# Two edge stages of a graph network: keys and values of a tile four chunks sooner, the second layer's closing steps of a tile in fewer steps

## The chip, the cores and the metric

The kernel runs on one core of a Trainium2 chip. The metric is the device time of one execution in microseconds. Before the change three runs took 2850.37, 2851.22 and 2853.70 us; the median is 2851.22.

A core has engines with a queue of instructions each, which run in order and meet through semaphores: PE (TensorE, matmuls and turns of 128x128 blocks), DVE (VectorE), ACT (ScalarE), POOL (GpSimd) and SP (SyncE). In this kernel POOL issues gathers of table rows, SP issues most other loads, and ACT the stores of the edge stages.

## The reference, cut to what matters

6250 nodes with 256 features, 100000 edges sorted by target and one loop per node. `x` is normalised to `xn`; two graph attention layers with 4 heads follow, and beside them one linear attention without softmax, whose keys and values are normalised per head:

```python
def gat_conv(x, src, dst, W, a_src, a_dst, b):
    h = (x @ W).reshape(-1, H, C)
    e = leaky_relu(alpha_s[src] + alpha_d[dst], 0.2)
    ex = exp(e - segment_max(e, dst)[dst])
    alpha = ex / segment_sum(ex, dst)[dst]
    return segment_sum(h[src] * alpha[:, :, None], dst).reshape(-1, H * C) + b
x0 = relu(gat_conv(xn, src, dst, W1, ...))
x2 = gat_conv(x0, src, dst, W2, ...)

k, v = _inst_norm_lastdim(k), _inst_norm_lastdim(v)      # 8 heads of 64
dots = einsum('bhnd,bhne->bhde', k, v)
out = einsum('bhnd,bhde->bhne', q, dots) / n             # then Wout, + bout

x = x + x2 + out
x = x + _L0_ffn_ref(_layernorm(x))                       # 16 experts, best 2, gate logits x @ gate_w
```

## The kernel before, in words

The program is a row of stages with a barrier of all engines behind each. Two of them, one per layer, are built by `gat_edges` (L771) and are the stages that the change touches. In between stands a short stage that bounds the logits; after the second layer come the ordering of tokens by expert, the experts and the last norm.

An edge stage walks 98 chunks of 1024 edges; two chunks go with one tile of 128 nodes, so there are 49 tiles. For a chunk SP loads its source numbers (`load`, L902) and the targets' codes (`load_codes`, L908), POOL gathers 8 x 128 table rows into one of three slots (L950), PE fetches the targets' terms (`targets`), DVE forms the logits (`edge_logits`, L1009), ACT their exponentials (`exps`, L1143), DVE scales the gathered rows (`edge_scale`, L1028), PE adds them up by target (`add`, L1266), and DVE puts the sums into the accumulator (`gain`, L1036). POOL's gather of a chunk waits until the scaling of the chunk three before it is done. A few matmuls without use (L1250, L1258) fill pauses of PE.

For each tile further steps follow. In both layers DVE takes the reciprocal of the denominators (`denominators`, L1045) and ACT divides (`divide`, L1156). Then, in the first layer, PE turns the result (`fin_turn`, L1296), ACT applies relu (L1176), PE projects it for the second layer (`project`, L1302), ACT copies it out (`copies`, L1184) and stores it. Beside that runs a second row of steps which depends on the node's own features alone: load of the transposed rows (`load_x`, L920), values and keys on PE (L1274, L1280), squares on ACT (L1164), sums on DVE (L1061), square roots on ACT (L1170), scaled keys on DVE (L1070) and their products with the values, summed over all tiles on PE (`dots`, L1288). When all tiles are through, DVE and PE make the mixing matrix from the products (L1080 to L1085, L1313, L1318). In the second layer PE mixes (`mix`, L1326 to L1329: features, mixing matrix, bias and the divided sums in one bank), DVE takes the statistics (`stats`, L1091) and keeps a copy (`with_beta`, L1098), ACT takes the root (L1203), DVE makes the factors (`scales`, L1102), ACT normalises (`normalise`, L1209) and stores, PE turns the tile (`fin_turn`, L1335), ACT copies it (`xf_turned`, L1214), PE computes the gate logits (`gates`, L1342), and ACT copies these out (L1218). When the last are there, DVE adds the gate's bias (L1113) and picks the experts.

The order on each engine is written by `chunks` (L858) with `skewed` (L90). Each engine has a list of pairs of an offset and a step. At time t of its own program it runs, in the list's order, each step for chunk t - offset; a step marked `True` belongs to tiles and runs only where t - offset is even. Head and tail are written out, six chunks in the middle make the body of a loop. So an offset sets beside which chunk's steps a step stands, and the list sets the order inside a chunk; semaphores do the rest.

Of the kernel before, what the change touches and what calls it, by code (L numbers as in the profile page):

```python
# [56 lines left out]
def hold(eng, sem, value, tick):  # L57

    eng.wait_ge(sem, value)
    eng.sem_inc(tick, 1)  # L60
# [24 lines left out]
def rows_of(i):  # L85

    return LAST if isinstance(i, int) and i == NT - 1 else P


def skewed(eng, n, period, head, tail, stages):  # L90

    most, least = max(o for o, _ in stages), min(o for o, _ in stages)
    start = head + most
    turns = max(0, n - tail + least - start) // period

    def whole(t):  # L100
        for o, step in stages:
            if 0 <= t - o < n:
                step(t - o, (t - o) % period, (t - o) // period)
    for t in range(min(least, 0), start):
        whole(t)
    if turns:
        with eng.Fori(0, turns) as m:  # L107
            for r in range(period):
                for o, step in stages:
                    k = start + r - o  # L110
                    step(m * period + k, k % period, m + k // period)
    for t in range(start + turns * period, n + most):
        whole(t)
# [657 lines left out]
def gat_edges(nc, layer, srcp, table, idx, G, ahead, codes_d, partition, iota, acc, own, peak, parts, windows, attention, last, sem):  # L771
# [6 lines left out]
    with ExitStack() as ctx:  # L778
# [79 lines left out]
        def chunks(eng, begin, end, *stages):  # L858


            rounds = eng.value_load(passes[0:1, 0:1], min_val=1, max_val=NT + 1)
            with eng.Fori(0, rounds) as r:
                def told(step):
                    return lambda c, k, u: step(r * NC + c, c, k % SLOTS, k % 2, r * len(range(k % SLOTS, NC, SLOTS)) + u * 2 + k // SLOTS)

                def tile_of(step):

                    def even(c, k, u):
                        if k % 2 == 0:
                            b = k // 2  # L870
                            step(r * NT + (u * SLOTS + b), u * SLOTS + b, b, r * len(range(b, NT, SLOTS)) + u)
                    return even
                begin(r)
                skewed(eng, NC, 2 * SLOTS, 2, 2, [(o, tile_of(step) if by_tile else told(step)) for o, step, *by_tile in stages])
                end(r)
            return rounds
# [4 lines left out]
        def new_pass(eng):  # L881
            return lambda r: hold(eng, s["pass"], r * 3 + 3, s["tick"])

        def new_dest(eng):
            return lambda r: hold(eng, s["dests"], r + 1, s["tick"])

        def both_new(eng):
            def begin(r):
                new_pass(eng)(r)
                new_dest(eng)(r)  # L890
            return begin
# [4 lines left out]
        @block.sync  # L896
        def _(sp):
            def next_load(r):
                hold(sp, s["logits"], r * NC + NC + SLOTS, s["tick"])
                sp.dma_start(idx[:, 0, :], srcp[0:CE].rearrange("(p t) -> p t", t=KT)).then_inc(s["idx_in0"], 16)  # L900

            def load(g, c, q, par, use):  # L902
                if isinstance(c, int) and c == 0:
                    return
                hold(sp, s["logits"], g + 1, s["tick"])
                sp.dma_start(idx[:, q, :], srcp[ds(c * CE, CE)].rearrange("(p t) -> p t", t=KT)).then_inc(s[f"idx_in{q}"], 16)

            def load_codes(g, c, q, par, use):  # L908
                hold(sp, s["hotT"], g + 1, s["tick"])
                sp.dma_start(codes[:, par, :], codes_d[ds(c * CE, CE)].rearrange("(o e) -> o e", o=1).to_broadcast([P, CE])).then_inc(s[f"codes_in{par}"], 16)  # L910

            sp.sem_inc(s["stored"], PER_STORE)
            if attention:
                for kc in range(2):
                    sp.dma_start(bias[:, kc:kc + 1], a["L0_gnn_b1"][kc * P:(kc + 1) * P].rearrange("(p o) -> p o", o=1)).then_inc(s["constants"], 16)

                def load_x(t, i, b, use):
                    sp.wait_ge(s["values_ps"], t + 1)
                    sp.wait_ge(s["keys_ps"], t + 1)
                    sp.dma_start(xnT[b], xnT_d[ds(i, 1), :, :].rearrange("o p f -> (o p) f")).then_inc(s[f"xn_in{b}"], 16)  # L920

                rounds = chunks(sp, new_pass(sp), next_load, (0, load), (-1, load_codes), (1, load_x, True))
            else:
                sp.dma_start(bias[0:1, 0:C], a["L0_gnn_b2"].rearrange("(o c) -> o c", o=1)).then_inc(s["constants"], 16)
                sp.dma_start(bias[0:1, C:2 * C], a["L0_mix_bout"].rearrange("(o c) -> o c", o=1)).then_inc(s["constants"], 16)
                sp.dma_start(beta, a["L0_ffn_beta"].rearrange("(o c) -> o c", o=1).to_broadcast([P, C])).then_inc(s["constants"], 16)
                sp.dma_start(gate, a["L0_ffn_gate_w"].rearrange("(k p) e -> p k e", p=P)).then_inc(s["constants"], 16)
                for rows in (xf_d, moe_d):
                    sp.dma_start(rows[NT * P:(NT + 1) * P, 0:C], mixM[:, 0, :]).then_inc(s["constants"], 16)
                sp.dma_start(gbias, a["L0_ffn_gate_b"].rearrange("(o e) -> o e", o=1).to_broadcast([P, NX])).then_inc(s["constants"], 16)  # L930

                def load_x(t, i, b, use):
                    n = rows_of(i)
                    sp.wait_ge(s["mixed"], t + 1)
                    sp.dma_start(x[b][0:n, :], a["x"][ds(i * P, n), :]).then_inc(s[f"x_in{b}"], 16)
                    sp.dma_start(xnT[b], xnT_d[ds(i, 1), :, :].rearrange("o p f -> (o p) f")).then_inc(s[f"x_in{b}"], 16)

                rounds = chunks(sp, new_pass(sp), next_load, (0, load), (-1, load_codes), (6, load_x, True))
            hold(sp, s["stored"], rounds * (PER_STORE * NT) + PER_STORE, s["tick"])

        @block.gpsimd
# [34 lines left out]
        def _(dve):  # L976
# [81 lines left out]
            if attention:  # L1058
# [13 lines left out]
                key = Chain(dve, s["key"])  # L1072
                dve.sem_inc(s["kvsum"], 1)
                dve.sem_inc(s["ks"], 1)
                rounds = chunks(dve, both_new(dve), next_pass, (1, edge_logits), (1, placed), (1, edge_scale), (6, keys, True), (-1, one_hot), (3, gain), (5, denominators, True), (5, sums, True))

                hold(dve, s["dots"], rounds * NT + SLOTS, s["tick"])
                for hp in range(4):
# [7 lines left out]
            else:  # L1086
# [20 lines left out]
                dve.wait_ge(s["constants"], 112)  # L1107
                dve.tensor_tensor(bias[0:1, 0:C], bias[0:1, 0:C], bias[0:1, C:2 * C], ALU.add).then_inc(s["bias"], 1)
                dve.memset(acc[:, NT + 2, :], 4.0).then_inc(s["yb"], 1)
                rounds = chunks(dve, both_new(dve), next_pass, (1, edge_logits), (1, placed), (8, scales, True), (1, edge_scale), (-1, one_hot), (3, gain), (5, denominators, True), (7, stats, True), (7, with_beta, True))  # L1110

                hold(dve, s["gate_logits"], rounds * NT + 1, s["tick"])
                steps.link(dve.tensor_tensor(logits, logits, gbias.rearrange("p (t e) -> p t e", t=1).to_broadcast([P, NT, NX]), ALU.add))  # L1113
# [24 lines left out]
        def _(act):  # L1138
# [20 lines left out]
            if attention:  # L1159
# [31 lines left out]
                act.sem_inc(s["vs"], 1)  # L1191
                act.sem_inc(s["out"], 4)
                act.wait_ge(s["constants"], 32)
                chunks(act, new_dest(act), nothing, (9, store, True), (6, roots, True), (1, exps), (6, divide, True), (5, squares, True), (7, relu, True), (8, copies, True))
            else:
                act.wait_ge(s["codes_in1"], 16)
                act.wait_ge(s["idx_in2"], 16)
# [26 lines left out]
                act.sem_inc(s["xf"], 1)  # L1224
                act.sem_inc(s["xfT"], 1)
                act.sem_inc(s["gate_logits"], 1)
                chunks(act, new_dest(act), nothing, (9, store, True), (8, root, True), (1, exps), (13, gates, True), (11, xf_turned, True), (6, divide, True), (8, normalise, True))
                act.wait_ge(s["gap"], 1)
                act.activation(gap[:], gap[:], ACT.Exp).then_inc(s["exp"], 1)

# [1 line left out]
        def _(pe):  # L1232
# [19 lines left out]
            def after_placed(n):  # L1252

                def step(g, c, q, par, use):
                    pe.wait_ge(s["acc"], g * 2 + 2)
                    pe.wait_ge(s["hotf"], g + 1)
                    for _ in range(n):
                        pe.matmul(psA[:, q, 0:C], ident[:], wext[:, 0, 0:C] if attention else mixM[:, 0, :], start=True, stop=True)  # L1258
                return step
# [9 lines left out]
            if attention:  # L1269
# [29 lines left out]
                def project(t, i, b, use):  # L1299
                    pe.wait_ge(s["relu"], t + 1)  # L1300
                    for kc in range(2):
# [3 lines left out]
                pe.sem_inc(s["values_ps"], SLOTS)  # L1305
                pe.sem_inc(s["keys_ps"], SLOTS)
                pe.sem_inc(s["projected"], 1)
                chunks(pe, nothing, nothing, (1, targets), (2, add), (7, fin_turn, True), (7, dots, True), (8, project, True),
                       (1, after_logits), (5, keys, True), (4, values, True), (1, after_placed(2)))

                pe.wait_ge(s["end"], 8)
                for hp in range(4):
# [7 lines left out]
            else:  # L1320
# [17 lines left out]
                def gates(t, i, b, use):  # L1338
                    pe.wait_ge(s["xfT"], t + 2)
                    pe.wait_ge(s["gate_logits"], t + 1)  # L1340
                    for kc in range(2):
# [3 lines left out]
                pe.sem_inc(s["gated"], 1)  # L1345
                pe.wait_ge(s["constants"], 112)
                pe.wait_ge(s["bias"], 1)
                chunks(pe, nothing, nothing, (1, targets), (2, add), (12, gates, True), (10, fin_turn, True), (7, mix, True),
                       (1, after_logits), (1, after_placed(3)))


# [464 lines left out]
```

## Time and profile before

| | us |
|---|---|
| median of 3 runs | 2851.22 |
| profiled execution | 2856.6 |
| its span | 2855.0 |
| first edge stage, first gather to mixing matrix | 189.91 to 1211.14 |
| second edge stage, first gather to last gate logits | 1238.42 to 2257.66 |
| POOL busy | 1867.3 (65%) |
| PE busy | 2212.2 (77%) |
| DVE busy | 1832.7 (64%) |
| ACT busy | 924.3 (32%) |

The span is the time from the first to the last instruction of the profiled execution. A share is a mean over all stages, which are bound by different engines; the two edge stages make up over 2000 of the 2855 us.

### The profile page before, as it was taken

The page shows a single profiled execution, that of the slowest core. Times are in us where ns is not written, and L with a number is a line of the kernel's source. Part 1 is how long each engine was busy: PE and PEld are TensorE (multiplying, and loading weights), DVE is VectorE, ACT ScalarE, POOL GpSimd, SP SyncE. Part 2 cuts the span into 40 slices and gives each one's busy share as a digit, 9 for nine tenths or more (in the row PEclk, how much of TensorE's full clock was granted, in tenths as well). Part 3 has the DMA queues.
Part 4 walks back from the last instruction along what each step waited for, and adds up shares of the span by engine and source line. Part 5 has one row for each costly group of instructions (what it writes and reads, how often), then busy time and mean ns, then how long its engine had stood idle before and what let it go on. Part 6 is the DMA issues. An engine that isn't in the chain of part 4 may idle for free. (4 is left out here: it accounts for less than half of the span.)

```text
span 2855.0 us, 54407 instructions
## 1 busy us (share of the span) xinstructions
PE 2212.2 (77%) x11635; PEld 1734.9 (61%) x11636; DVE 1832.7 (64%) x4388; ACT 924.3 (32%) x2254; POOL 1867.3 (65%) x1934
## 2 busy tenths in 40 slices
PE   1727787777777787737888888888888569999986
PEld 0525555555555555536666666666666359999985
DVE  5656767777777777566666666666666475555546
ACT  0512333333333333301222222222222244444436
POOL 0247777777777777467777777777777116666654
PEclk9969999999999999969999999999999679999998
DMA  3735555555555555255555565555565255555545
GB/s 70 221 107 141 147 147 147 147 145 145 145 145 146 145 149 142 74 193 157 158 161 161 156 161 154 162 154 162 157 163 158 70 150 103 103 104 104 101 86 187
DMA packets 274988, 401.57 MB, mean 141 GB/s; under 512 B 91136, under 2 KB 187799, under 8 KB 274905
## 3 DMA queue, kind: packets, MB, share of 16 engines
q0 software_dynamic: 102496, 253.89, 36.1%
q1 hardware_dynamic: 128745, 101.18, 13.4%
q10 hardware_dynamic: 43680, 45.76, 4.9%
q8 instruction: 24, 0.39, 0.1%
q14 instruction: 43, 0.35, 0.0%
HBM read 346.42 MB, written 54.62 MB: 140 GB/s over the span
## 5 line engine op out<-in xcount | busy, mean ns | idle before, releaser
L950 POOL DMA_INDIRECT gathered<-table,idx x1568 | 1501.5, 958 | 508.0 <-issue 451.5
L1266 PE MATMUL psA_e<-scaled,hotf 128*128 128x260 f32 x3136 | 745.8, 391 | 43.5 <-issue 38.9
L1266 PEld LDWEIGHTS psA_e<-scaled,hotf 128*128 128x128 f32 x3136 | 587.6, 192 | 132.7 <-issue 47.9
L1146 ACT ACTIVATE scaled<-t_e 128x32 f32<-128x32 f32 x196 | 45.0, 230 | 735.6 <-DVE t_e L1017 734.6
L1679 POOL DMA_INDIRECT moe_d<-xscaled,xtarget x113 | 179.3, 1587 | 125.8 <-DVE xtarget L1623 53.7
L1028 DVE TENSOR_TENSOR scaled<-gathered,psDW_e 128x2048 f32<-128x2048 f32 x98 | 223.5, 2281 | 25.7 <-ACT psDW_e L1147 25.7
L1021 DVE TENSOR_TENSOR hotf<-psA_e,code_r 128x1024 f32<-128x1024 f32 x196 | 239.6, 1222 | 0.0
L1028 DVE TENSOR_TENSOR scaled<-gathered,psW_e 128x2048 f32<-128x2048 f32 x98 | 223.5, 2280 | 22.8 <-ACT psW_e L1147 22.8
L1651 PEld LDWEIGHTS xpsH<-xxT,w1e 128*128 128x128 f32 x1808 | 221.1, 193 | 6.2 <-ACT xxT L1580 0.4
L1660 PE MATMUL xpsO<-w,hidT 128*128 x904 | 217.5, 384 | 9.2 <-DVE hidT L1612 9.0
L1651 PE MATMUL xpsH<-xxT,w1e 128*128 128x128 f32 x1808 | 221.8, 276 | 0.0
L1250 PE MATMUL psD_e<-mixM,ident 128*128 128x256 f32 x392 | 121.3, 437 | 117.2 <-DVE t_e L1017 117.0
L1036 DVE SCALAR_TENSOR_TENSOR acc<-psA_e,lower,acc 128x260 f32 x196 | 95.7, 488 | 151.6 <-issue 151.3
L1612 DVE TENSOR_SCALAR hidT<-xpsH,b1T 128x128 f32<-128x128 f32 x452 | 127.3, 344 | 93.6 <-issue 43.3
L1660 PEld LDWEIGHTS xpsO<-w,hidT 128*128 128x128 f32 x904 | 163.3, 191 | 31.8 <-issue 13.4
L1258 PE MATMUL psA_e<-mixM,ident 128*128 128x256 f32 x588 | 177.4, 446 | 5.0
L1015 DVE TENSOR_TENSOR z_e<-both_e,gathered 128x32 f32<-128x32 f32 x196 | 37.8, 193 | 218.4 <-DMA gathered<-table,idx 209.6
L1146 ACT ACT_TABLE_LOAD x95 | 121.9, 1283 | 171.8 <-DVE t_e L1017 142.7
L1250 PEld LDWEIGHTS psD_e<-mixM,ident 128*128 128x128 f32 x392 | 75.9, 207 | 143.0 <-DVE t_e L1017 134.3
L1258 PEld LDWEIGHTS psA_e<-mixM,ident 128*128 128x128 f32 x588 | 127.2, 225 | 47.2 <-issue 26.9
L1280 PE MATMUL psKV<-w 128*128 128x512 f32 x196 | 102.0, 645 | 65.2 <-DVE t_e L1017 65.1
L1274 PE MATMUL psKV<-w 128*128 128x512 f32 x196 | 99.2, 629 | 66.6 <-DVE t_e L1017 66.6
(322 smaller groups left out, 3372.1 us busy)
## 6 DMA issues: line engine op xcount, KB each, us to landing
w<-codes_d SPq DMA_DIRECT2D x196, 256.0 KB
gathered<-table,idx POOLq DMA_INDIRECT x1584
w<-in_L_ffn_w ACTq DMA_DIRECT2D x8, 2048.0 KB, 19.8
xb<-in_L_ffn_b SPq DMA_DIRECT2D x113, 128.0 KB
table<-acc POOLq DMA_DIRECT2D x49, 130.0 KB
table<-acc ACTq DMA_DIRECT2D x49, 130.0 KB
xnT_d<-xnT ACTq DMA_DIRECT2D x49, 128.0 KB, 1.8
w<-xnT_d SPq DMA_DIRECT2D x49, 128.0 KB
```

Of the source, the lines that this page charges most:

```text
L950: pool.indirect_dma_start(out=G[:, q, k, :], out_offset=None, in_=table, in_offset=bass.IndirectOffsetOnAxis(ap=idx[:, q, k:k + 1], axis=0 ...
L1021: dve.tensor_tensor(hotf[:, q, :, :], psA[:, q, 512 - P:512].rearrange("p (k f) -> p k f", k=1).to_broadcast([P, KT, P]), code_r[:, ds(c * ...
L1028: dve.tensor_tensor(scaled[:, par, :, 0:C].rearrange("p k (h c) -> p k h c", h=H), f, w, ALU.mult).then_inc(s["scaled"], 1)
L1146: act.activation(scaled[:, par, :, C:GW], t[:], ACT.Exp).then_inc(s["weights"], 1)
L1250: pe.matmul(psD_bank[:, 256:256 + C], ident[:], mixM[:, 0, :], start=True, stop=True)
L1258: pe.matmul(psA[:, q, 0:C], ident[:], wext[:, 0, 0:C] if attention else mixM[:, 0, :], start=True, stop=True)
L1266: ins = pe.matmul(psA[:, q, 0:GW], hotf[:, q, k, :], scaled[:, par, k, :], start=(k == 0), stop=(k == KT - 1))
L1280: ins = pe.matmul(psKV[:, 0, :], xnT[b][:, kc * P:(kc + 1) * P], wkvT[:, kc, 0, :], start=(kc == 0), stop=(kc == 1))
L1612: dve.tensor_scalar(hidT[:, q % 2, k * P:(k + 1) * P], psH[:, q % 2, k * P:(k + 1) * P], b1T[:, ds(e, 1), k:k + 1].rearrange("p o k -> p ( ...
L1651: ins = pe.matmul(psH[:, q % 2, k * P:(k + 1) * P], w1e[:, q % 2, kc, k * P:(k + 1) * P], xT[:, q % 2, kc, :], start=(kc == 0), stop=(kc = ...
L1660: ins = pe.matmul(psO[:, q % 2, 0:C], hidT[:, q % 2, k * P:(k + 1) * P], w2[:, ds(e, 1), k, :].rearrange("p o f -> p (o f)"), start=(k == ...
L1679: pool.indirect_dma_start(out=moe_d, out_offset=bass.IndirectOffsetOnAxis(ap=target[:, q % 2:q % 2 + 1], axis=0), in_=scaled[:, q % 2, :], ...
```

## The change

It alters only offsets and, in one list, the order; no operation is added, dropped or resized.

First layer: the offset of each of the eight steps of keys and values falls by four chunks: loading 1 to -3, values 4 to 0, keys, squares and sums 5 to 1, roots and scaled keys 6 to 2, products 7 to 3. Dividing, turning, relu, projecting, copying and storing stay.

Second layer: loading 6 to 4, mixing 7 to 6, statistics and copy 7 to 6, roots, scales and normalising 8 to 7, store 9 to 8, turn 10 to 9, copy of the turned tile 11 to 9, gates on PE 12 to 10, gates on ACT 13 to 11. The division keeps 6. On ACT, division and copy of the turned tile now stand ahead of the exponentials of the same time, where they stood behind.

```diff
 # SP, first and second layer
-(0, load), (-1, load_codes), (1, load_x, True)
+(0, load), (-1, load_codes), (-3, load_x, True)
-(0, load), (-1, load_codes), (6, load_x, True)
+(0, load), (-1, load_codes), (4, load_x, True)
 # DVE, first and second layer
-(1, edge_logits), (1, placed), (1, edge_scale), (6, keys, True), (-1, one_hot), (3, gain), (5, denominators, True), (5, sums, True)
+(1, edge_logits), (1, placed), (1, edge_scale), (2, keys, True), (-1, one_hot), (3, gain), (5, denominators, True), (1, sums, True)
-(1, edge_logits), (1, placed), (8, scales, True), (1, edge_scale), (-1, one_hot), (3, gain), (5, denominators, True), (7, stats, True), (7, with_beta, True)
+(1, edge_logits), (1, placed), (7, scales, True), (1, edge_scale), (-1, one_hot), (3, gain), (5, denominators, True), (6, stats, True), (6, with_beta, True)
 # ACT, first and second layer
-(9, store, True), (6, roots, True), (1, exps), (6, divide, True), (5, squares, True), (7, relu, True), (8, copies, True)
+(9, store, True), (2, roots, True), (1, exps), (6, divide, True), (1, squares, True), (7, relu, True), (8, copies, True)
-(9, store, True), (8, root, True), (1, exps), (13, gates, True), (11, xf_turned, True), (6, divide, True), (8, normalise, True)
+(8, store, True), (7, root, True), (6, divide, True), (9, xf_turned, True), (1, exps), (11, gates, True), (7, normalise, True)
 # PE, first and second layer
-(1, targets), (2, add), (7, fin_turn, True), (7, dots, True), (8, project, True), (1, after_logits), (5, keys, True), (4, values, True), (1, after_placed(2))
+(1, targets), (2, add), (7, fin_turn, True), (3, dots, True), (8, project, True), (1, after_logits), (1, keys, True), (0, values, True), (1, after_placed(2))
-(1, targets), (2, add), (12, gates, True), (10, fin_turn, True), (7, mix, True), (1, after_logits), (1, after_placed(3))
+(1, targets), (2, add), (10, gates, True), (9, fin_turn, True), (6, mix, True), (1, after_logits), (1, after_placed(3))
```

How the instructions stand, at three places. On SP at the start of the first layer's edge stage, before (L910 loads codes, L906 source numbers, L920 transposed rows):

```order
L59 ISA
L910 DMA w<-codes_d 128x1024
L59 REGISTER_ALU
L910 DMA w<-codes_d 128x1024
L906 DMA idx<-srcp 128x8
```

and now:

```order
L918 ISA
L920 DMA w<-xnT_d 128x256
L59 ISA
L910 DMA w<-codes_d 128x1024
L918 REGISTER_ALU
L920 DMA w<-xnT_d 128x256
L59 REGISTER_ALU
L910 DMA w<-codes_d 128x1024
L906 DMA idx<-srcp 128x8
```

Two loads of transposed rows stand ahead of the first load of source numbers; the one that stood behind it is now for a later tile.

On PE at the end of the same stage, after the last chunk's rows were added up, before (psKV are keys and values, psF turned and projected tiles, psM the products):

```order
L1294 ISA
L1296 MATMUL psF<-ident,w 128x128 x2
L1288 MATMUL psM<-w 128x128 x4
L1280 MATMUL psKV<-w 128x512 x2
L1302 MATMUL psF<-wext,w 128x264 x2
L1271 ISA
L1272 REGISTER_ALU
L1274 MATMUL psKV<-w 128x512 x2
```

and now, from the same turn to the barrier:

```order
L1294 ISA
L1296 MATMUL psF<-ident,w 128x128 x2
L1284 REGISTER_ALU
L1288 MATMUL psM<-w 128x128 x4
L1302 MATMUL psF<-wext,w 128x264 x2
L1294 ISA
L1296 MATMUL psF<-ident,w 128x128 x2
L1302 MATMUL psF<-wext,w 128x264 x2
```

Keys and values of the last tiles no longer stand between the turns and the projections; one set of products is left there, and it is the last tile's.

On ACT in the second layer's loop, before (L1203 roots, L1146 and L1147 exponentials, L1156 division, L1214 copy of the turned tile, L1218 gate logits):

```order
L1218 ISA
L1218 ACTIVATE w<-psG 128x16
L1213 REGISTER_ALU
L1214 ACTIVATE w<-psX_1 128x256
L1203 ACT_TABLE_LOAD
L1203 ACTIVATE w<-w,eps 128x1
L1144 ISA
L1145 REGISTER_ALU
L1146 ACT_TABLE_LOAD
L1146 ACTIVATE scaled<-t_e 128x8x4
L1147 ACTIVATE psW_e<-t_e 128x32
```

and now:

```order
L1203 ACT_TABLE_LOAD
L1203 ACTIVATE w<-w,eps 128x1
L1214 ACTIVATE w<-psX_1 128x256
L1144 ISA
L1145 REGISTER_ALU
L1146 ACT_TABLE_LOAD
L1146 ACTIVATE scaled<-t_e 128x8x4
L1147 ACTIVATE psW_e<-t_e 128x32
L1218 ISA
L1218 ACTIVATE w<-psG 128x16
```

The copy of the turned tile stands between the root and the table load of the next exponentials; the gate logits stand behind these.

## Rows read from the trace of the kernel before

**Rows 1.** Groups by line, first edge stage, 240:1160 us: busy, mean | idle.

```profile
L950 POOL DMA_INDIRECT gathered<-table,idx x733 | 696.9, 951 | 223.4 <-issue 210.0 <-DVE scaled L1028 12.2 <-DMA idx<-srcp 1.2
```

**Rows 2.** The same view, second edge stage, 1300 to 2190 us.

```profile
L950 POOL DMA_INDIRECT gathered<-table,idx x709 | 674.3, 951 | 216.1 <-issue 205.1 <-DVE scaled L1028 8.2 <-DMA idx<-srcp 2.7
```

**Rows 3.** Waits of DVE, 1300 to 2190 us: total, times, longest.

```profile
DVE z_e L1015 <- DMA gathered<-table,idx: 99.8, 41, 4.0
```

**Rows 4.** Timeline, one tile of the second layer: start, length, engine, line [idle before].

```profile
1741.91 1.28 ACT L1146 ACT_TABLE_LOAD   x1 [1.72 <-DVE t_e L1017]
...
1743.20 0.23 ACT L1146 ACTIVATE scaled<-t_e 128x32 f32<-128x32 f32 x1
...
1743.56 2.29 DVE L1028 TENSOR_TENSOR scaled<-gathered,psW_e 128x2048 f32<-128x2048 f32 x1 [0.32 <-ACT psW_e L1147]
...
1750.04 1.03 PE L1326 MATMUL psY<-mixM,w1e 128*128 128x256 f32 x4
...
1752.29 0.38 ACT L1214 ACTIVATE w<-psX 128x256 f32<-128x256 f32 x1
...
1752.59 1.03 PE L1250 MATMUL psD_e<-mixM,ident 128*128 128x256 f32 x4
...
1752.73 2.27 DVE L1028 TENSOR_TENSOR scaled<-gathered,psW_e 128x2048 f32<-128x2048 f32 x1
...
1755.11 3.75 PE L1266 MATMUL psA_e<-scaled,hotf 128*128 128x260 f32 x16
...
1758.63 0.18 DVE L1045 RECIPROCAL rden<-acc 128x4 f32 x1 [0.99 <-DVE acc L1036]
...
1758.69 0.52 PE L1342 MATMUL psG<-w 128*128 128x16 f32 x4
...
1759.05 0.42 PE L1335 MATMUL psX<-ident,w 128*128 128x128 f32 x2
```

**Rows 5.** Timeline, end of the first layer's edge stage.

```profile
1180.65 0.38 PE L1296 MATMUL psF<-ident,w 128*128 128x128 f32 x2
...
1183.68 1.02 ACT L1164 ACTIVATE w<-psKV 128x1024 f32<-128x1024 f32 x1 [8.60 <-PE psKV L1280]
...
1189.24 0.49 DVE L1036 SCALAR_TENSOR_TENSOR acc<-psA_e,lower,acc 128x260 f32 x1 [0.61 <-issue]
...
1197.95 0.69 PE L1296 MATMUL psF<-ident,w 128*128 128x128 f32 x2 [1.53 <-ACT dtab L1185]
...
1198.71 0.62 ACT L1176 ACTIVATE w<-psF,w 128x128 f32<-128x128 f32 x2 [0.81 <-PE psF L1296]
...
1200.14 1.97 PE L1302 MATMUL psF<-wext,w 128*128 128x264 f32 x4
...
1202.37 0.39 ACT L1184 ACTIVATE acc<-psF 128x260 f32 x1 [3.04 <-PE psF L1302]
...
1210.45 0.69 DVE L1085 COPY mixM<-psM 128x512 f32<-128x512 f32 x1 [3.81 <-PE psM L1318]
```

**Rows 6.** Timeline, end of the second layer's edge stage.

```profile
2235.87 2.05 PE L1326 MATMUL psY<-mixM,w1e 128*128 128x256 f32 x4 [3.21 <-ACT w L1209]
...
2243.24 1.06 ACT L1156 ACTIVATE w<-acc,rden 128x64 f32 x4 [0.94 <-DVE acc L1098]
...
2244.90 2.05 PE L1326 MATMUL psY<-mixM,w1e 128*128 128x256 f32 x4 [2.66 <-ACT w L1209]
...
2252.41 0.56 ACT L1209 ACTIVATE w<-psY,w 128x256 f32<-128x256 f32 x1 [1.07 <-DVE w L1104]
...
2256.41 1.03 PE L1342 MATMUL psG<-w 128*128 128x16 f32 x4 [0.47 <-ACT w L1214]
...
2257.81 0.97 DVE L1113 TENSOR_TENSOR w<-w 128x784 f32<-128x784 f32 x1 [4.36 <-ACT w L1218]
```

**Rows 7.** Timeline, start of the first layer's edge stage.

```profile
184.90 13.43 DVE L992 TENSOR_TENSOR acc<-acc 128x3136 f32<-128x3136 f32 x4 [0.43 <-ACT acc L1141]
...
189.91 2.65 POOL L950 DMA_INDIRECT gathered<-table,idx  x1 [6.70 <-DMA idx<-srcp]
```

More of the change, by code:

```diff
@@ L920, in load_x @@
                     sp.dma_start(xnT[b], xnT_d[ds(i, 1), :, :].rearrange("o p f -> (o p) f")).then_inc(s[f"xn_in{b}"], 16)
-                rounds = chunks(sp, new_pass(sp), next_load, (0, load), (-1, load_codes), (1, load_x, True))
+                rounds = chunks(sp, new_pass(sp), next_load, (0, load), (-1, load_codes), (-3, load_x, True))
             else:
@@ L936, in load_x @@
                     sp.dma_start(xnT[b], xnT_d[ds(i, 1), :, :].rearrange("o p f -> (o p) f")).then_inc(s[f"x_in{b}"], 16)
-                rounds = chunks(sp, new_pass(sp), next_load, (0, load), (-1, load_codes), (6, load_x, True))
+                rounds = chunks(sp, new_pass(sp), next_load, (0, load), (-1, load_codes), (4, load_x, True))
             hold(sp, s["stored"], rounds * (PER_STORE * NT) + PER_STORE, s["tick"])
@@ L1074, in _ @@
                 dve.sem_inc(s["ks"], 1)
-                rounds = chunks(dve, both_new(dve), next_pass, (1, edge_logits), (1, placed), (1, edge_scale), (6, keys, True), (-1, one_hot), (3, gain), (5, denominators, True), (5, sums, True))
+                rounds = chunks(dve, both_new(dve), next_pass, (1, edge_logits), (1, placed), (1, edge_scale), (2, keys, True), (-1, one_hot), (3, gain), (5, denominators, True), (1, sums, True))
                 hold(dve, s["dots"], rounds * NT + SLOTS, s["tick"])
@@ L1109, in _ @@
                 dve.memset(acc[:, NT + 2, :], 4.0).then_inc(s["yb"], 1)
-                rounds = chunks(dve, both_new(dve), next_pass, (1, edge_logits), (1, placed), (8, scales, True), (1, edge_scale), (-1, one_hot), (3, gain), (5, denominators, True), (7, stats, True), (7, with_beta, True))
+                rounds = chunks(dve, both_new(dve), next_pass, (1, edge_logits), (1, placed), (7, scales, True), (1, edge_scale), (-1, one_hot), (3, gain), (5, denominators, True), (6, stats, True), (6, with_beta, True))
                 hold(dve, s["gate_logits"], rounds * NT + 1, s["tick"])
@@ L1193, in _ @@
                 act.wait_ge(s["constants"], 32)
-                chunks(act, new_dest(act), nothing, (9, store, True), (6, roots, True), (1, exps), (6, divide, True), (5, squares, True), (7, relu, True), (8, copies, True))
+                chunks(act, new_dest(act), nothing, (9, store, True), (2, roots, True), (1, exps), (6, divide, True), (1, squares, True), (7, relu, True), (8, copies, True))
             else:
@@ L1226, in _ @@
                 act.sem_inc(s["gate_logits"], 1)
-                chunks(act, new_dest(act), nothing, (9, store, True), (8, root, True), (1, exps), (13, gates, True), (11, xf_turned, True), (6, divide, True), (8, normalise, True))
+                chunks(act, new_dest(act), nothing, (8, store, True), (7, root, True), (6, divide, True), (9, xf_turned, True), (1, exps), (11, gates, True), (7, normalise, True))
                 act.wait_ge(s["gap"], 1)
@@ L1307, in _ @@
                 pe.sem_inc(s["projected"], 1)
-                chunks(pe, nothing, nothing, (1, targets), (2, add), (7, fin_turn, True), (7, dots, True), (8, project, True),
-                       (1, after_logits), (5, keys, True), (4, values, True), (1, after_placed(2)))
+                chunks(pe, nothing, nothing, (1, targets), (2, add), (7, fin_turn, True), (3, dots, True), (8, project, True),
+                       (1, after_logits), (1, keys, True), (0, values, True), (1, after_placed(2)))
                 pe.wait_ge(s["end"], 8)
@@ L1347, in _ @@
                 pe.wait_ge(s["bias"], 1)
-                chunks(pe, nothing, nothing, (1, targets), (2, add), (12, gates, True), (10, fin_turn, True), (7, mix, True),
+                chunks(pe, nothing, nothing, (1, targets), (2, add), (10, gates, True), (9, fin_turn, True), (6, mix, True),
                        (1, after_logits), (1, after_placed(3)))
```

## Prediction

> **What bounds the kernel now.** I read the busy shares at the head of the profile first: POOL is busy 65%, PE 77%, DVE 64%, and none of them is full over the span. So I asked stage by stage, with the groups by line. Both edge stages belong to POOL. In 920 us of the first, 733 indirect gathers took 696.9 us, and POOL's idle time of 223.4 us is almost all "issue", about 0.3 us between one gather and the next [rows 1]; 696.9 + 223.4 = 920.3, which is the whole window. In 890 us of the second it is 674.3 + 216.1 = 890.4 [rows 2]. One gather costs 890.4 / 709 = 1.256 us, so a chunk (8 gathers) 10.05 us and a tile (two chunks) 20.1 us. POOL waited for DVE for 8.2 us in all there. DVE, on the other side, waited 99.8 us for gathered rows [rows 3]: about 2.2 us for each of some 44 tiles. So DVE, ACT and PE follow, and a step moved among them costs nothing as long as their own circle closes within 20.1 us per tile and a chunk is freed before POOL comes back to its slot three chunks later.
>
> What POOL doesn't cover are the two ends, after the last gather, where the steps of the last tiles run one after another, and the first microseconds of a stage. There the change can give or take.
>
> **The change, part by part.** *First layer, inside the stage.* Load, values, keys, squares, sums, roots, key scaling and products of a tile all move by the same four chunks, an even number, so each keeps its neighbours in a chunk's list on every engine. Each chunk still holds the same instructions, for a tile two further on. No DMA is added; only the tile that it loads differs. Cost 0, hidden under POOL [rows 1].
>
> *First layer, end.* Before, keys and values of the last two tiles are computed after the last gather, between the output steps of tiles 46 to 48. ACT stood 8.60 us until the key matmul of tile 47 let it square [rows 5]; the turned hidden state of tile 46 was ready soon after 1180.65 and waited behind that. The sums for tile 47 also held DVE in its queue, so the last chunk's accumulation came at 1189.24. The turn of tile 48 starts at 1197.95, the end of the stage is the mixing matrix at 1210.45 + 0.69 = 1211.14. Afterwards none of that stands there, and one tile's round remains: turn 0.69, relu 0.62, projection 1.97, copies (0.39 and a small one, about 0.46 together), with some 0.45 of hand-overs, 4.2 us with PE at the lower of its two clock levels, as in these rows, and about 3.1 us at the upper, at which the turn took 0.38 [rows 5]. Two rounds from 1180.65 to 1181.8 (up to 1.1 later if the last accumulation on PE runs at the lower clock, since the value matmul before it goes) put the turn of tile 48 at 1187 to 1190, middle 1188.7: 9.2 us sooner. Behind it, the products (L1288) of tile 48 go from between relu, which ended at 1199.33, and projection at 1200.14: 0.8 us. The final products and copies after that stay. Sum 10 us; bounds 7 and 12.
>
> *First layer, start.* SP now issues two loads of transposed rows (128 KB each) ahead of the first index load, on which POOL's first gather waited until 189.91 [rows 7]. With 256 KB more in front of it, beside two code lists of 256 KB each that stand there already, I estimate that list 1 to 2 us later. That gather, 2.65 us long, stood under four DVE multiplies of 13.43 / 4 = 3.36 us each that began at 184.90: it ended at 192.56, 0.94 (a usual gather's length, 951 ns in [rows 1]) after the boundary between the second and third at 191.62, as if it had only run in the gap. If it still starts before 191.62, nothing is lost, otherwise one gather, 1.25 us; both ends are kept and I take 0.6.
>
> *Second layer, inside the stage.* Here steps change parity, and a new circle forms: the division (ACT) feeds the mixing of the same chunk (PE), which stands before that chunk's filler matmuls and so before the next accumulation; behind that comes the turn, and the copy of the turned tile now stands on ACT ahead of the next exponentials, for which DVE's scaling waits. From the reciprocal's end R [rows 4, 6]: hand-over 0.2, division 1.06, hand-over 0.1; mixing to filler 1752.59 - 1750.04 = 2.55; filler to accumulation 1755.11 - 1752.59 = 2.52; accumulation to the next step 1758.69 - 1755.11 = 3.58; turn 0.42 and hand-over 0.05; copy 0.38; from the exponential's table load to the scaling 1743.56 - 1741.91 = 1.65; from the scaling to the end of the next reciprocal 1758.81 - 1752.73 = 6.08. Sum 18.6 us against 20.1. It closes with 1.5 to spare, so POOL keeps the pace and I cost it at 0. Before, the circle left about 2.2 [rows 3]. Behind the waiting copy stand the exponentials, a gate copy and the normalising; behind the waiting mixing the fillers and the next targets. Without POOL's cover each us over 20.1 costs 1 us in each of some 45 tiles. Below zero there is nothing either: POOL isn't sped up.
>
> On the table load the Trainium skill, ScalarE: Activation LUTs, section What ACT_TABLE_LOAD costs, speaks against the change: 1283 ns and a drain of about 1380 ns for every switch. The trace shows the 1.28, and the exponential at 1743.20, 0.01 behind its end [rows 4]; no drain is seen. With the drain the circle would be an estimated 20.0, and nothing left.
>
> *Second layer, end.* Mixing of tile 47 started at 2235.87, of tile 48 at 2244.90, its normalised rows were ready at 2252.41 + 0.56 = 2252.97, and the logits were complete at 2257.81 [rows 6]: 4.84 us in which PE did the gate of tile 47, the turn of 48 and the gate of 48, with an ACT copy before each gate. Afterwards the copy and gate of 47 come before the normalising, and behind it remain one turn (0.7, as in [rows 5]), one copy (0.38), one gate (1.03) and hand-overs: 2.6. That is 2.2 less. Mixing of tile 47 starts up to 2 us sooner, for its division no longer waits for the tile before to be scaled, but then scales, reciprocal, normalising and store lie between it and the next division, so I keep only 0.5 of it. Sum 2.7; bounds 1 and 4. In these rows PE is at the lower level, 1.2 GHz: L1326 takes 2.05 for 1.03 in [rows 4]. I leave it so.
>
> **Sum.** -10 + 0.6 - 2.7 = -12.1 us. The profiled execution took 2856.6 (span 2855.0), so 2844.5 on its own scale. It lies 5.4 over the median of the runs, 2851.2; the same difference taken from the median gives 2839.1.
>
> **Rivals.** *A: the circle of the second layer becomes the bound (slower).* Place: ACT's exponentials behind the turned copy, DVE's scaling behind these. It decides from 20.1 us per tile, that is 1.5 over my sum. For it: mixing at the lower clock takes twice 2.55, which alone makes it 21.2, and PE now has a pause before each mixing, from the gate's end to the division's, about 1 us. Against: that pause is shorter than the 3.21 us before the slow L1326 [rows 6]. Price: 1.1 x 45 = 50 us, 2889; with half of the tiles at the lower clock the mean is 19.9 and nothing is lost. By the Trainium skill's drain (same section of ScalarE: Activation LUTs) the half-slow case would be an estimated 21.3 and 2893; with no drain in the rows it has 0.02 of A's chance.
>
> *B: keys and values didn't matter at the first end.* The output steps of the last tiles could be as long without them, since projection, copies and turn form a chain of their own; then only the second end counts: 2851.2 + 0.6 - 2.7 = 2849. For it: the last three rounds are serial anyway. Against: the 8.60 us.
>
> *C: half of it comes back.* PE, less busy, runs all of the first end at the lower clock, the index load costs a whole gather, and the second end gives 1: -7 + 1.3 - 1 = -6.7, 2844.5.
>
> **How the numbers follow.** What a measurement here can tell from no change is about 0.2%, 5.7 us. My forecast has 0.60 and C 0.14, both faster; B has 0.12 and is no change, A 0.14 and is slower. Faster 0.74, same 0.12, slower 0.14. The likeliest case is 2839, with its own range 2836 to 2845. To 2852 it takes in B; only A, and ends that are better than both bounds, lie outside.
>
> **What would show it.** Gathers in the middle of both stages at 1.256 us each as before, and DVE still waiting for gathered rows in the second layer, though less than 2.2 us per tile. No squares on ACT behind the first layer's last scaling, and the mixing matrix about 10 us closer to it. At the second end one gate behind the last normalising. POOL waiting for DVE's scaling in the middle of the second layer, or the time from last gather to mixing matrix unchanged, would prove me wrong.

## The result, and the profile of the changed kernel

The changed kernel takes 2870.48 us (median of 4 runs, 2865.11 to 2871.92), the kernel before 2851.06 (4 runs). The ratio is 1.006, with a 95% interval of 1.0048 to 1.0073: slower, where 2839 was predicted. The profiled execution took 2865.11 us (span 2863.5).

The first layer did what was forecast. Groups by line, 240 to 1160 us, as in [rows 1]:

```profile
L950 POOL DMA_INDIRECT gathered<-table,idx x735 | 697.0, 948 | 223.9 <-issue 211.1 <-DVE scaled L1028 11.3 <-DMA idx<-srcp 1.5
```

Timeline of its start and end (start, length, engine, line, what is done, idle time before), as in [rows 5, 7]:

```profile
191.22 1.32 POOL L950 DMA_INDIRECT gathered<-table,idx  x1 [8.02 <-DMA idx<-srcp]
192.85 2.98 POOL L950 DMA_INDIRECT gathered<-table,idx  x1 [0.31 <-issue]
...
1187.16 0.69 PE L1296 MATMUL psF<-ident,w 128*128 128x128 f32 x2 [0.77 <-ACT dtab L1185]
...
1199.04 0.69 DVE L1085 COPY mixM<-psM 128x512 f32<-128x512 f32 x1 [3.81 <-PE psM L1318]
```

Before, the second gather stood at the same place:

```profile
192.86 2.98 POOL L950 DMA_INDIRECT gathered<-table,idx  x1 [0.31 <-issue]
```

The gathers keep their pace, and nothing is lost at the start. The turn of the last tile is at 1187.16 where it was at 1197.95, and the mixing matrix at 1199.04 where it was at 1210.45: 11.4 us sooner. So the 19 us that were lost lie behind it, and 11 more that were given away there.

Groups by line, 1300 to 2190 us, as in [rows 2]:

```profile
L950 POOL DMA_INDIRECT gathered<-table,idx x697 | 660.3, 947 | 230.6 <-issue 206.2 <-DVE scaled L1028 21.0 <-DMA idx<-srcp 3.4
```

Twelve gathers fewer in the same 890 us, and longer waits for VectorE, 21.0 us for 8.2. The waits of DVE there (total, times, longest), as in [rows 3]:

```profile
DVE both_e L1012 <- issue: 88.5, 15, 7.5
...
DVE scaled L1028 <- ACT psW_e L1147: 36.0, 41, 1.5
...
DVE z_e L1015 <- DMA gathered<-table,idx: 10.7, 7, 2.3
```

DVE waited 99.8 us for gathered rows before and 10.7 now. In their place stand 88.5 us, in 15 times, for nothing that the profile shows ("issue"); before, that row held 2.7. Thirteen of the fifteen are long, 6.3 to 7.5 us with a mean of 6.8. One of them, in the timeline of DVE:

```profile
1623.52 0.42 DVE L1098 TENSOR_TENSOR acc<-psY,w 128x256 f32 x1 [0.60 <-issue]
1630.27 0.36 DVE L1012 TENSOR_REDUCE both_e<-psD_e 128x64 f32<-128x192 f32 x1 [6.33 <-issue]
1630.87 0.19 DVE L1015 TENSOR_TENSOR z_e<-both_e,gathered 128x32 f32<-128x32 f32 x1 [0.24 <-DVE both_e L1012]
```

The next one ends at 1692.23, the fifth of such a row (from 1506.13) at 1754.57, so one comes every 62.1 us: once in 6 chunks, which is one pass through the loop that `skewed` builds on DVE (called a turn of the loop from here on; it has nothing to do with the turn of a tile). Each stands at that loop's back branch: ahead of it ran the last step of the loop's body (L1098), behind it the first (L1012). The DMA queues from 1300 to 2190 us (queue: packets, MB, share) say what goes on then; q14 is the queue that loads instructions:

```profile
q14 instruction: 70, 0.57, 0.2%
```

The kernel before moved 7 such packets in the same 890 us. From one stall to the next there are five, and three of the five fall into the stall itself (1624 to 1630.3 us in the one shown). So instructions of the loop are fetched anew in each turn.

The second end, as in [rows 6]:

```profile
2241.79 1.07 ACT L1156 ACTIVATE w<-acc,rden 128x64 f32 x4 [1.84 <-issue]
...
2252.76 1.06 ACT L1156 ACTIVATE w<-acc,rden 128x64 f32 x4 [1.76 <-issue]
...
2261.41 0.56 ACT L1209 ACTIVATE w<-psY,w 128x256 f32<-128x256 f32 x1 [0.73 <-DVE w L1104]
...
2264.91 0.97 DVE L1113 TENSOR_TENSOR w<-w 128x784 f32<-128x784 f32 x1 [2.46 <-ACT w L1218]
```

From the last normalising's end to the logits it is 2.94 us instead of 4.84. But one division follows the other by 10.97 us, where the mixings of before, each right behind its division, were 9.03 apart.

### The profile page after: what moved, and what is told of

It is laid out like the page before. It is cut to its first block and busy times, and to the rows that moved or that the text cites. A ratio compares the mean times of both kernels' runs of the same rounds, so it can differ in the third digit from the quotient of the medians.

```text
span 2863.5 us, 54563 instructions
## 1 busy us (share of the span) xinstructions
PE 2201.2 (77%) x11635; PEld 1741.0 (61%) x11636; DVE 1838.7 (64%) x4388; ACT 929.1 (32%) x2255; POOL 1861.8 (65%) x1934
## 5 line engine op out<-in xcount | busy, mean ns | idle before, releaser
L1266 PE MATMUL psA_e<-scaled,hotf 128*128 128x260 f32 x3136 | 760.9, 397 | 69.1 <-issue 40.3
L1266 PEld LDWEIGHTS psA_e<-scaled,hotf 128*128 128x128 f32 x3136 | 597.4, 195 | 161.2 <-issue 72.3
L1028 DVE TENSOR_TENSOR scaled<-gathered,psW_e 128x2048 f32<-128x2048 f32 x98 | 223.7, 2282 | 50.0 <-ACT psW_e L1147 50.0
L1028 DVE TENSOR_TENSOR scaled<-gathered,psDW_e 128x2048 f32<-128x2048 f32 x98 | 223.7, 2282 | 25.6 <-ACT psDW_e L1147 25.6
L1156 ACT ACTIVATE w<-acc,rden 128x64 f32 x392 | 103.7, 335 | 280.9 <-DVE rden L1045 269.9
L1660 PEld LDWEIGHTS xpsO<-w,hidT 128*128 128x128 f32 x904 | 162.8, 190 | 32.4 <-issue 14.5
L1146 ACT ACTIVATE scaled<-t_e 128x32 f32<-128x32 f32 x196 | 44.7, 228 | 415.4 <-DVE t_e L1017 413.9
L1258 PE MATMUL psA_e<-mixM,ident 128*128 128x256 f32 x588 | 163.1, 419 | 1.0
```

What stands on the lines that cost most here:

```text
L1028: dve.tensor_tensor(scaled[:, par, :, 0:C].rearrange("p k (h c) -> p k h c", h=H), f, w, ALU.mult).then_inc(s["scaled"], 1)
L1146: act.activation(scaled[:, par, :, C:GW], t[:], ACT.Exp).then_inc(s["weights"], 1)
L1156: ins = act.activation(hidden[:, h * CH:(h + 1) * CH], acc[:, ds(d, 1), h * CH:(h + 1) * CH].rearrange("p o f -> p (o f)"), ACT.Copy, scal ...
L1266: ins = pe.matmul(psA[:, q, 0:GW], hotf[:, q, k, :], scaled[:, par, k, :], start=(k == 0), stop=(k == KT - 1))
L1660: ins = pe.matmul(psO[:, q % 2, 0:C], hidT[:, q % 2, k * P:(k + 1) * P], w2[:, ds(e, 1), k, :].rearrange("p o f -> p (o f)"), start=(k == ...
```

## The experiments

Why is code fetched anew? The change adds no instruction, but an offset also sets how many steps `skewed` writes out ahead of a loop. Counted in DVE's program, the head of the second-layer loop is instruction 1643 before (260 instructions long) and 1618 after (258). Theory 1: the place alone makes the stall and the loss. Theory 2: the new order is too long a circle (a chain of steps through several engines that closes on itself once per tile). All extra waits below are on a semaphore that has long been there; two of them make one instruction, run once. The stage below is the time from the first scaling of the second layer (L1028) to the last. The first four, with the edits (the lists themselves stand under The change):

```diff
e1: the kernel after, L1107
-                dve.wait_ge(s["constants"], 112)
+                [dve.wait_ge(s["constants"], 112) for _ in range(51)]
e2: the kernel before, same line
+                [dve.wait_ge(s["constants"], 112) for _ in range(205)]
e3: the kernel before with the new lists of the first layer (L922, L1075, L1194, L1308, L1309)
e4: the kernel before with the new lists of the second layer (L938, L1110, L1227, L1348)
```

> The kernel after, with 50 more waits on a semaphore that is already there, ahead of VectorE's second-layer loop: 25 instructions, run once, which put the head of that loop at the same place of VectorE's program as in the kernel before (instruction 1643 instead of 1618). Loop and schedule are unchanged. Theory 1 (the back branch of the loop has to fetch its instructions anew at this one place): the 7.29 us before L1012 once a turn are gone (its 'issue' wait of 88.5 us in 1300:2190 falls to some 3 us), the instruction queue q14 moves some 7 packets in the stage instead of 70, and the time falls from 2870.5 by about 25 us to 2840 to 2848 us. Theory 2 (the new order of division, mixing, turn and exponentials is a longer circle): no change, 2868 to 2873 us.

Measured: 2840.8 us, ratio to before 0.9973 (0.9964 to 0.9982). The L1012 row is 2.7 us again and q14 moved 6 packets. By the medians 30 us are the loop's place; of the 23 between the two profiled executions the stage has 19.5 (979.7 to 960.1) and the end behind it 2.6.

> The kernel before, with 204 more waits at the same place: 102 instructions, so that its second-layer loop on VectorE stands as the loop of the kernel after does (25 + 102 is one short of 128 instructions further). Schedule unchanged. Theory 1: a stall of about 7 us once a turn of the loop appears, 14 or so times, with q14 packets beside each, and the time rises by 15 to 25 us to 2866 to 2876 us. Theory 2: 2851 us, and at most 5 us more for the waits themselves.

Measured: 2861.47, ratio 1.0037 (1.0024 to 1.005). The stall is there (DVE waits, 1300 to 2190):

```profile
DVE both_e L1012 <- issue: 51.7, 14, 4.2
...
DVE z_e L1015 <- issue: 30.0, 13, 2.6
```

81.7 us in all, but theory 1 missed what it costs. The stage took 959.1 us where the kernel before took 961.4: with the old schedule the same stall is free. Of the 11.9 us that the kernel takes longer, 10.24 are the extra instructions themselves, in the timeline of DVE:

```profile
1253.36 0.41 DVE L1108 TENSOR_TENSOR w<-w 1x256 f32<-1x256 f32 x1 [10.24 <-issue]
```

> The kernel before with the first layer's four lists of the change (L922, L1075, L1194, L1308/1309); second layer as before. Both theories: the first layer's end falls by 11 us (mixing matrix L1085 at 1199 us instead of 1210.45) and the time by as much: 2838 to 2842 us, a ratio of 0.996. A third, that the time gained there is given back at the start of the second layer: 2846 to 2852 us.

Measured: 2841.74, ratio 0.9974 (0.9965 to 0.9983). The mixing matrix is at 1198.8 us. The gain is there without the second layer's part, and nothing is given back.

> The kernel before with the second layer's four lists of the change (L938, L1110, L1227, L1348); first layer as before. Its loop on VectorE stands 10 instructions nearer to the start than in the kernel after. Theory 1: no stall at the back branch, and the time is within 4 us of the kernel before, 2848 to 2855 us. Theory 2: the slower order shows itself without the first layer, 2866 to 2876 us.

Measured: 2848.21, ratio 0.9994 (0.9985 to 1.0003), no stall (L1012: 2.4 us), stage 960.4 us. So the new schedule alone costs nothing either. It needs both.

How narrow is the bad place? Again the kernel after, with range(3), range(257) and range(255) in L1107: 1, 128 and 127 instructions more.

> The kernel after with 2 more waits at the same place: 1 instruction (loop head of VectorE's second layer at 1619 instead of 1618). Theory 1a (the loop of 258 instructions stalls only where it touches four blocks of 128 instructions, that is, where its first one is the last of a block): one instruction is enough, no stall, 2838 to 2846 us. Theory 1b (instructions are fetched ahead, so a loop that merely comes close to the fourth block stalls too, and the bad places are several): the stall stays, 2864 to 2873 us.

> The kernel after with 256 more waits at the same place: 128 instructions (head at 1746). If code is fetched in blocks of 128 instructions, the loop stands in its block as in the kernel after and stalls: 14 times some 7 us, 2864 to 2876 us. If the blocks are of 256, it is half a block away and does not stall: 2838 to 2848 us, of which up to 5 us may be the waits themselves.

> The kernel after with 254 more waits at the same place: 127 instructions (head at 1745), with blocks of 128 the place one instruction ahead of that of the kernel after. Theory 1a with blocks of 128: the loop then fills its blocks to the last instruction and touches three, so there is no stall, 2838 to 2848 us. Theory 1b, or a place of the kernel after that is not the very last of its block: the stall is there, 2864 to 2876 us. With blocks of 256: no stall.

Measured: one instruction is enough, 2840.11 us (0.9963, 0.9952 to 0.9975); with 128 it stalls, 2875.12 (1.0084, 1.0067 to 1.0101); with 127 it does not, 2854.81 (1.0015, 1.0005 to 1.0024), of which 12.65 us are the waits, more than the 5 us allowed for above. The waits of DVE and queue rows, 1300 to 2190 us, of 128 more:

```profile
DVE both_e L1012 <- issue: 88.0, 14, 7.2
```

```profile
q14 instruction: 69, 0.57, 0.2%
```

and of 127 more:

```profile
DVE both_e L1012 <- issue: 2.4, 14, 0.2
```

So the bad place comes back after 128 instructions, and what fits is code in blocks of 128 with 1618 the last of one: 1 + 128 + 128 + 1 = 258, four blocks. One instruction either way, and it is three. Where blocks begin follows here from the runs alone, and smaller blocks that divide 128, such as 64, would give the same three answers; none was tried. The Trainium skill, Runtime: NRT & Kernel Launch, section Instruction fetch mechanics, says that a taken branch to code outside what is held waits for a fetch, and the traces agree (5 packets per turn, stalls of 6.3 to 7.5 us); it gives two blocks of 256 instructions as what is held. With blocks of 256, 128 more would have put the loop out of harm, and it did not.

What remained open was why a stall of 6 to 7 us is free in one schedule and costs 18 to 20 us of stage in the other. Theory 3: GpSimd needs 60.3 us for the 6 chunks of a turn (6 x 10.05, [rows 2]), and a stall costs what turn and stall together are over that. The chain of scalings of the kernel after closes in 18.59 us per pair of chunks where GpSimd isn't waited for, at L1028 in its timeline:

```profile
1633.25 2.29 DVE L1028 TENSOR_TENSOR scaled<-gathered,psW_e 128x2048 f32<-128x2048 f32 x1 [0.32 <-ACT psW_e L1147]
...
1649.79 0.38 ACT L1214 ACTIVATE w<-psX 128x256 f32<-128x256 f32 x1 [2.21 <-PE psX L1335]
1650.19 1.28 ACT L1146 ACT_TABLE_LOAD   x1
...
1651.84 2.29 DVE L1028 TENSOR_TENSOR scaled<-gathered,psW_e 128x2048 f32<-128x2048 f32 x1 [1.22 <-ACT psW_e L1147]
```

3 x 18.6 + 6.3 = 62.1, and 62.1 is the period of the stalls. The sum is rough: the three pairs from 1633.25 on took 18.59, 19.20 and, with the stall, 24.17 us, and with the mean stall of 6.8 it would be 62.5. To test it I moved entries in ACT's list (L1227), which leaves DVE's program alone (only the entries that move are shown, without their `True`):

```diff
after:   (6, divide), (9, xf_turned), (1, exps), (11, gates)
e8, e9:  (1, exps), (11, gates), (9, xf_turned), (6, divide)      (e9: with range(3) in L1107)
e11, e12: (6, divide), (1, exps), (9, xf_turned), (11, gates)     (e12: with range(3) in L1107)
e10: e4 with range(21) in L1107, which puts its loop at 1618
```

> The kernel after with ScalarE's second-layer list (L1227) in the order of before: exponentials, gates, turn, division instead of division, turn, exponentials, gates; the offsets of after. VectorE's program is unchanged, so its loop keeps its place and the 6 to 7 us at each back branch stay. Theory 3 (the stall costs time only because the circle of 18.6 us per pair of chunks, which runs through this order, fills the turn: 3 x 18.6 + 6.3 = 62.1 us against the 60.3 us that GpSimd needs for 6 chunks): with the exponentials first the circle is shorter, the stall is hidden as in the second experiment, and the stage from the first to the last scaling L1028 falls from 979.7 to 960 to 965 us, the time to 2842 to 2855 us. Theory 1 by itself (the stall always costs what it costs): stage 975 to 980 us, 2864 to 2872 us.

> The same with 2 more waits (1 instruction) ahead of VectorE's second-layer loop, so that there is no stall. Theory 3 and theory 1: GpSimd's 20.1 us per pair bound the stage in either order, so it is that of the fifth experiment, 2838 to 2843 us, within 3 us of 2840; at the end of the second layer the old order may give a us or two either way. If the old order were the better one in itself: below 2837 us.

Measured: 2925.94 us (1.0282, 1.026 to 1.0303) and 2861.52 (1.0045, 1.0032 to 1.0058). I had the direction of this order wrong. The waits of PE and DVE in the second of them, which has no stall:

```profile
PE psY L1326 <- ACT w L1156: 108.7, 44, 3.4
```

```profile
DVE both_e L1012 <- PE psD_e L1243: 65.7, 39, 2.6
```

With the division behind the exponentials, the mixing, a chunk sooner by the new offset, holds PE 2.5 us in each pair ahead of the next targets, and DVE waits for these. PE's clock has a part in it: 0.87 (e8) and 0.86 (e9) of full speed were granted from 1300 to 2190 us, 0.96 in e5, and in e9, behind a wait of 2.28 us, the mixing at 1616.09 us took 4.2 us to the filler behind it, where [rows 4] have 2.55. How much of the loss is the clock was not tried apart. A pair then takes 20.34 us (1606.71 to 1708.43, five pairs), over GpSimd's 20.1. The circle bounds, and three quarters of the stall are paid: stage 975.6 us without it, 1037.0 with it, 61.4 more for stalls of 83.1 us. The price follows the circle, as theory 3 has it, but by a kernel that was meant to show the opposite.

> The kernel with the second layer's part of the change alone (as the fourth experiment), and 20 more waits, 10 instructions, which put the head of VectorE's second-layer loop at 1618, as in the kernel after. If it takes the new second-layer schedule and the bad place together, whatever the first layer does: the stage from the first to the last scaling L1028 rises from 960.4 to 977 to 982 us, and the time by 19 to 22 us (1 us of it for the waits) to 2866 to 2871 us. If the first layer's part had a share: less than 2860 us.

Measured: 2873.69 us (1.0093, 1.0077 to 1.0109), some 27 us over the kernel before, more than expected. Its stage took 980.7 us, 19.3 more than before; what makes up the rest is not shown. The first layer has no share in the loss.

> The kernel after with one move in ScalarE's second-layer list (L1227): the turn xf_turned goes behind the exponentials, the division stays ahead of them. VectorE's program and the stall at its back branch are as in the kernel after. Theory 3 (what a stall costs is what turn of the loop and stall are over the 60.3 us of GpSimd): the exponentials of one chunk of each pair no longer wait for the turn (1649.2 to 1649.8 and the copy of 0.4 us, about 0.9 us per pair, 2.8 us per turn of three), so the turn with its stall falls from 61.85 to about 59 us, under 60.3: stage 960 to 966 us, time 2841 to 2850 us. If some other wait takes that place, as in the eighth experiment: 2865 us or more.

> The same with 1 instruction more ahead of the loop, so without the stall. GpSimd bounds the stage in theory 3: as the fifth experiment, 2837 to 2843 us. If the move makes a new wait: above 2846 us.

Measured: 2840.87 us (0.9976, 0.9965 to 0.9987) with the stall, 2838.91 (0.9964, 0.995 to 0.9978) without. The stall is still in the first (DVE waits, queue, 1300 to 2190 us):

```profile
DVE both_e L1012 <- issue: 86.8, 15, 7.2
...
DVE scaled L1028 <- ACT psW_e L1147: 13.4, 42, 0.3
```

```profile
q14 instruction: 70, 0.57, 0.2%
```

and costs nothing: GpSimd has its pace again, in the groups by line:

```profile
L950 POOL DMA_INDIRECT gathered<-table,idx x711 | 673.9, 948 | 216.6 <-issue 205.3 <-DVE scaled L1028 7.6 <-DMA idx<-srcp 3.7
```

The turn's copy left the path, as DVE's and ACT's timeline shows:

```profile
1628.25 2.29 DVE L1028 TENSOR_TENSOR scaled<-gathered,psW_e 128x2048 f32<-128x2048 f32 x1 [0.32 <-ACT psW_e L1147]
...
1644.46 1.28 ACT L1146 ACT_TABLE_LOAD   x1 [1.72 <-DVE t_e L1017]
...
1646.01 0.37 ACT L1214 ACTIVATE w<-psX 128x256 f32<-128x256 f32 x1
1646.11 2.29 DVE L1028 TENSOR_TENSOR scaled<-gathered,psW_e 128x2048 f32<-128x2048 f32 x1 [0.32 <-ACT psW_e L1147]
```

17.86 us per pair instead of 18.59: with the mean stall of 6.6 us 3 x 17.86 + 6.6 = 60.2, just under 60.3. Its stage took 958.7 us. Little is left of the spare: between 1550 and 2160 us DVE waited for no gathered row.

The periods of the stalls say the same without the sum. From one stall to the next it was 60.1 us in e2, 60.3 in e11, 62.1 in the kernel after and 66.3 in e8. What each is over 60.3, times 13 stalls, gives 0, 0, 23 and 78 us. Against the 959.7 us of e5, which has no stall, the stages were no longer in e2 and e11 (959.1 and 958.7), 20 us longer in the kernel after and 77 in e8 (979.7 and 1037.0).

e1, e5, e11 and e12 are versions of the change that beat both kernels, the one before by 0.24 to 0.37%; which of the four is best is not shown, since their intervals overlap.

## Why the prediction was wrong

The step that failed is "Second layer, inside the stage", in the words "It closes with 1.5 to spare, so POOL keeps the pace and I cost it at 0".

- Its sum was right: 18.6 predicted, 18.59 in the trace, 19.20 in the pair behind it. So was the forecast that POOL would keep its pace while nothing else is added: without the stall the stage takes 959.7 us (e5) against 961.4.
- What it left out is that the spare is shared. 1.5 us per tile is 4.5 in a turn of the loop, and the new place of the loop put a stall of 6.8 (the mean) into each turn, 2.3 more. The turn came to 62.1, 1.8 over the 60.3; at 13 stalls that is 23 us, and the stage grew by 979.7 - 959.7 = 20 against the same schedule without the stall (e5), by 18.2 against the kernel before. That the difference is the lead that POOL had in its slots is my reading and was not tried apart. Nothing in the trace of before bears on the place: I counted instructions on each engine, not where they lie. The sign against it that the prediction had named came (POOL waited for DVE's scaling, 21.0 us for 8.2), and one that it had named for itself failed (DVE waited 10.7 us for gathered rows, not a little under 99.8).
- Rival A named the right place and the right point of decision (20.1 us per tile), but by PE's clock, at 50 us. PE's clock did not do it: 0.93 of full speed was granted in 1300 to 2190 us in the kernel after, and 0.94 in e11, which lost nothing. The fall of the clock that A feared is seen in e8 and e9 (0.87 and 0.86).
- First layer, end: 10 predicted, 11.4 in the profiled run. Over all traces the mixing matrix stands at 1196.8 to 1202.4 in the ten with the new first layer and at 1205.9 to 1210.5 in the four with the old, means 1199.3 and 1208.2: 9.0. The turn of the last tile was put at 1188.7 and came at 1187.16.
- First layer, start: 0.6 predicted, 0 measured, the lower bound. The first gather starts 1.3 us later (191.22 for 189.91), but still ahead of 191.62, and takes 1.32 us instead of 2.65, so the second starts at 192.85 where it started at 192.86. The prediction had this case too, in the words "nothing is lost", and took the middle of both.
- Second layer, end: 2.7 predicted. From the last scaling L1028 to L1113 it was 34.45 us before and is 32.4 and 32.6 without the stall (e4, e5): 1.9 gained. It is all behind the last division (14.57 before, 12.50 in e5); the 0.5 for an earlier mixing did not come, since a tile's round there, with scaling, normalising and store ahead of the next division, is 1.9 longer. In the kernel after the end gained nothing (34.8); in e11, which has the stall too, it is 30.3. In the times no gain of the second layer's part is clear of noise: e4 has 0.9985 to 1.0003.
- The sum without the stall: -12.1 predicted, 2840.11 - 2849.89 = -9.8 measured (e5). The forecast of 2839 us fits the change without the stall, not the kernel that was given.

## What to carry to other kernels

A schedule that is changed by offsets alone still moves code: count the loop's instructions and see where it begins, and if a loop is a little over 256 instructions (258 and 260 here), shift it by a few and measure again before judging the schedule. Look for a regular "issue" wait at a loop's back branch with packets of the instruction queue beside it. Compare the spare of a circle not with zero but with the sum of what a turn of the loop may have to absorb; the same stall was free at 17.9 us per pair of chunks, cost 18 to 20 us at 18.6, and 61 at 20.3, where a part of the circle was PE's clock.

## What the runs showed of the hardware

- A back branch of VectorE's loop that has to fetch its code takes 6.3 to 7.5 us in the kernel after (6.0 the shortest, in e8), with 5 q14 packets per turn, 3 of them in the stall. It happened with heads at 1618 and 1746 for the loop of 258 instructions and at 1745 for that of 260, and not with heads at 1608, 1619, 1643 and 1745 for the loop of 258 or at 1643 and 1653 for that of 260. A loop that touches four blocks of 128 instead of three is what fits all of these.
- A wait that is already met costs time on VectorE: 127 instructions of two waits each took 12.65 us (e7), 0.10 us apiece, and 102 took 10.24 (e2).
